# Turning x before the weights in the norm blocks of a twelve-stage decoder

## The reference

```python
def _layernorm(x, axis=-1, eps=1e-05):
    m = jnp.mean(x, axis=axis, keepdims=True)
    v = jnp.var(x, axis=axis, keepdims=True)
    return (x - m) / jnp.sqrt(v + eps)
```

## Time and profile before

| what | value |
|---|---|
| median of 3 runs | 2674.46 us (2674.36 to 2676.65) |
| time of the profiled execution | 2665.88 us |
| its span, first to last instruction | 2664.1 us |
| mean granted clock of PE over the span | 0.897 |
| PE busy | 2126.5 us, 80% |
| DVE busy | 1709.5 us, 64% |
| ACT busy | 1191.6 us, 45% |
| POOL busy | 588.5 us, 22% |

### The profile page before, as it was taken

How to read it: one execution, slowest core, us unless ns; L and a number is a source line. 1 busy time by engine, 2 the same in 40 slices (tenths; PEclk the granted TensorE clock), 3 DMA queues, 4 the chain that set the end, 5 groups by cost and what they waited for, 6 DMA issues and landing times. The chain is left out here.

```text
span 2664.1 us, 28164 instructions
## 1 busy us (share of the span) xinstructions
PE 2126.5 (80%) x10151; PEld 1326.3 (50%) x10181; DVE 1709.5 (64%) x2541; ACT 1191.6 (45%) x1889; POOL 588.5 (22%) x344
## 2 busy tenths in 40 slices
PE   5789889694699979979694888888778989272895
PEld 3456556584323325767541444444555654251574
DVE  5555455324677745632287999999845767857765
ACT  2334322100266653411065999999822236312330
POOL 3331112120242103012101756564101200000100
PEclk8889999697799998969897999999879989696996
DMA  6553120343554400034400000000111000000001
GB/s 125 86 88 41 61 95 0 107 158 126 101 79 64 48 20 2 1 108 161 131 32 32 1 1 1 0 1 1 65 59 36 1 1 0 0 8 21 0 1 38
DMA packets 107525, 126.69 MB, mean 48 GB/s; under 512 B 14823, under 2 KB 98676, under 8 KB 106357
## 3 DMA queue, kind: packets, MB, share of 16 engines
q1 hardware_dynamic: 96790, 110.17, 17.9%
q10 hardware_dynamic: 7712, 7.17, 0.9%
q0 software_dynamic: 2880, 7.48, 0.8%
HBM read 91.11 MB, written 33.29 MB: 47 GB/s over the span
## 5 line engine op out<-in xcount | busy, mean ns | idle before, releaser
L3274 DVE TENSOR_TENSOR_SCAN l2s_h<-l2w_aw 128x2048 f32<-128x2048 f32 x64 | 290.0, 4531 | 5.4 <-ACT l2s_rs L3394 5.4
L3202 PE MATMUL l2s_big<-g_xn,g_ident 128*128 128x512 f32 x512 | 258.4, 607 | 11.6 <-ACT g_xn L3387 6.4
L3358 POOL TENSOR_SCALAR l2w_aw<-l2w_aw 128x2048 f32<-128x2048 f32 x64 | 212.1, 3314 | 141.4 <-DVE l2w_aw L3266 136.2
L591 DVE TENSOR_REDUCE l1at_nm<-l1at_s 128x1 f32<-128x512 f32 x256 | 161.8, 683 | 65.3 <-PE l1at_s L441 64.4
L3194 PE MATMUL l2s_c_ps<-g_ident,l2s_h 128*128 128x128 f32 x1024 | 148.9, 279 | 55.7 <-ACT g_xn L3387 36.4
L3194 PEld LDWEIGHTS l2s_c_ps<-g_ident,l2s_h 128*128 128x128 f32 x1024 | 117.1, 141 | 146.8 <-issue 87.8
L691 ACT ACTIVATE g_xn<-l1at_s 128x512 f32<-128x512 f32 x256 | 143.5, 598 | 82.1 <-PE l1at_s L465 81.3
L3387 ACT ACTIVATE g_xn<-l2s_c_ps,l2s_ct 128x512 f32<-128x512 f32 x256 | 163.1, 690 | 15.9 <-PE l2s_c_ps L3194 15.7
L3380 ACT ACTIVATE l2w_aw<-l2s_dt,l2w_A 128x2048 f32<-128x2048 f32 x64 | 128.3, 2006 | 0.0
L591 DVE TENSOR_REDUCE l0at_nm<-l0at_s 128x2 f32<-128x384 f32 x128 | 69.7, 556 | 91.3 <-PE l0at_s L441 90.2
L3202 PEld LDWEIGHTS l2s_big<-g_xn,g_ident 128*128 128x128 f32 x512 | 82.0, 190 | 81.9 <-ACT g_xn L3387 59.2
(11 more groups left out here) (868 smaller groups left out, 4872.2 us busy)
## 6 DMA issues: line engine op xcount, KB each, us to landing
l1f_w<-in_L_ffn_w_dram SPq DMA_DIRECT2D x16, 1024.0 KB
l0f_w<-L_ffn_experts_inter_dram SPq DMA_DIRECT2D x7, 1024.0 KB
l0f_w<-n_L_ffn_experts_out_dram SPq DMA_DIRECT2D x7, 1024.0 KB
l0at_qs<-l0at_parts SPq DMA_DIRECT2D x18, 256.0 KB, 9.2
l0at_ks<-l0at_parts SPq DMA_DIRECT2D x18, 256.0 KB, 18.2
l1at_qs<-l1at_parts SPq DMA_DIRECT2D x18, 256.0 KB, 8.9
l1at_ks<-l1at_parts SPq DMA_DIRECT2D x18, 256.0 KB, 20.2
expert_rows<-g_zeros SPq DMA_DIRECT2D x1, 4096.0 KB, 12.8
```

The costliest lines, as they stand in the source:

```text
L591: V.tensor_reduce(nm[:, s % 2, qts[0]:qts[-1] + 1, r], s1[:, u % 3, 0:len(qts) * KEYS].rearrange("p (q k) -> p q k", k=KEYS), AX, ALU.max, ...
L3202: nc.tensor.matmul(acc[:, tb, :], ident[:], hCT[:, tb, :], start=n == 0, stop=n == NST - 1).then_inc(acc_done, 1)
L3274: V.tensor_tensor_scan(out=h_all[:, i % 2].rearrange("p c t -> p (c t)"), data0=dA[:, i % 2].rearrange("p c t -> p (c t)"), data1=wd[:, i ...
L3358: nc.gpsimd.tensor_scalar(wd[:, i % 3], wd[:, i % 3], 10.0, -10.0, ALU.min, ALU.max).then_inc(clipped, 1)
```

## The change

PE's list now has the pairs of x first and the groups of weights after them; ACT's list has, after the square root, its copies of the turned x first and those of the weights after them. Nothing is added or removed, and DVE, SP and the DMAs issued stay as they are. In l1a and l3c, without groups, the instruction lists are the same as before.

```diff
--- before.py
+++ after.py
@@ -274,15 +274,13 @@
                 for r in range(rounds):
                     act.wait_ge(var_ready, r + 1)
                     nc.scalar.activation(tmp[:], tmp[:], ACT.Sqrt).then_inc(std_ready, 1)
+                copy_turned(act, nc.scalar.copy, 0)
                 copy_blocks(act, nc.scalar.copy, groups, wt, wt_ready, wt_copied, 0, 1)
-                copy_turned(act, nc.scalar.copy, 0)
                 if loads[1::2]:
                     act.wait_ge(loaded[1], 16 * len(loads[1::2]))
 
             @block.tensor
             def _(pe):
-                turn_blocks(nc, pe, groups, wt, ident, loads, loaded, wt_ready, [wt_copied])
-
                 for g in range(TILES // 2):
                     pe.wait_ge(xn_ready, 2 * g + 2)
                     if g >= 4:
@@ -291,6 +289,7 @@
                         for v in range(2):
                             ins = nc.tensor.transpose(pt[:, g % 4, 2 * kc + v, :], xn[:, 2 * g + v, kc * P:(kc + 1) * P], ident[:])
                     ins.then_inc(tr_ready, 1)
+                turn_blocks(nc, pe, groups, wt, ident, loads, loaded, wt_ready, [wt_copied])
```

## The result

The changed kernel takes 2677.44 us (median of 22 runs, 2672.59 to 2686.59). The kernel before, run beside it, takes 2672.30 (22 runs, 2666.12 to 2677.30), which is 2.16 less than the 2674.46 of its first three runs. The ratio is 1.0020, with a 95% interval from 1.0014 to 1.0027: +5.1 us, between +3.7 and +7.2. It is slower, as forecast, but by half of the +10.6.

A forecast was written before the change was run, and what follows sets the result against it. DVE was taken to set the end of most norm blocks, hiding the weights' work. Upper-clock block terms of +6.57 us plus +4.0 for the clock gave +10.6 on 2674.46, so 2685.0 us, range 2678.0 to 2692.5.

The forecast's parts named there:

- Who ends a block, and that its end is paid: Norm blocks: DVE's last copy ends them, +8.36 after its first tensor_scalar; lengthening a block's last instruction is paid in full.
- The terms at the upper clock: Block-end changes with fast PE: l0a +2.48, l2a +4.21, l3a +0.99, l3b +0.50, l1b -1.61; sum +6.57 us.
- The 0.166: Spacing in us between starts of ACT's weight copies, read from l0a's 16 copies and used for l0a, l3a, l3b, l1b.
- I take two of five, +4.0: PE's clock in the five changed blocks: two run their last pairs at the lower clock, adding 4.0 us.
- The price: Cost of PE's lower clock in and behind one changed block, taken as 2.0 us.
- caught: State of a block whose last pairs PE turns at the lower clock; one to three such blocks forecast, chance 0.50.
- an even coin: Of l1a and l3c, blocks with the same lists, one had the lower clock; used as odds for the five changed blocks.
- the 2610.2 of the prediction: Time in l3c when PE's granted clock rose, about 2610.2 us, at the end of the first 20 transpositions.
- The base: Whole kernel: the blocks' terms were added to the median of runs before the change, 2674.46 us.
- The case of all five at the upper clock: Rival for the five changed blocks: none at the lower clock, +6.6 us, 2681.0 us; chance 0.20.
- Loads that land later in l1b: Rival: later landings in timed runs slow only the old order, up to 3.57 us in l1b; chance 0.10.
- The clock under transpositions: Norm blocks: a skill rule says transposing never raises the clock, so all five lag; l2a's trace disagreed, no share given.

The follow-up runs named there:

- ACT's list alone: Kernel before with ACT copying x ahead of the weights in l0a, l3a and l3b, PE's list unchanged; run twice, ratios 0.9997 and 1.0011.
- the filler: Kernel before with twenty transpositions of the identity put ahead of the pairs in l1a; ratio 1.0007.
- l1b alone: Kernel before with x ahead of the weights only in block l1b, on PE and ACT; ratio 0.9999.
- the caught one: Second run of the kernel before with x first only in l1b and the weights' copies there shared by ACT and DVE; ratio 0.9989.
- The second look at the changed kernel: The changed kernel run and profiled once more, unchanged, timed against the kernel before; ratio 1.0022.
- l2a alone: Kernel before with x ahead of the weights only in block l2a, on PE and ACT; run twice, ratios 1.0031 and 1.0021.
- l2a copied twice: Kernel before with x first only in l2a, and ACT copying each of its 28 weight blocks twice, first into a spare tile; ratio 1.0037.

## Why the prediction was wrong, point by point

**Who ends a block, and that its end is paid.** Right for the end of the block. In all thirteen profiles every block in the old order, l1b and l1a apart, ends at +8.36 to +8.38; ACT's copies behind it move the end one for one, and the next block's first instruction with it. "Paid in full" is not shown for the whole program: with ACT's list alone, both profiles had 1.6 of the 2.7 us back by the end.

**The terms at the upper clock.** Right, within 0.3 in each block and 0.4 in the sum (6.57 forecast, 6.16 read). l3a is the largest miss: four of its seven copies are of 128x64 and start 0.11 apart. The 0.166 itself has a wait in it: between the twelfth and the thirteenth copy of l0a before the change (15.36 to 15.65) ACT had nothing to copy yet. In the changed l0a the 16 copies start 0.157 apart (22.11 to 24.46). That the forecast for l0a is exact is therefore part luck, as its last copy lasted 0.46 and not 0.30.

**"I take two of five, +4.0."** This is the step that failed. The price was near (1.72 in the block against 2.0 taken; the 0.3 for what comes behind is not shown), how often it happens was not: in both profiles of the changed kernel the term is 0. In all profiles together, 16 blocks with weights ran with x first (five each in two profiles of the changed kernel, one each in six others), and one was caught. It is one of five in l1b and none of eleven in the other four. l3c, of the same shape, was at the upper clock for its last pairs in all thirteen. l1a is the odd one: its last pairs ran at the lower clock throughout in ten of thirteen, at the upper one in two, and fell between with the filler. I took one block of each kind for an even coin and spread it over five others; four of them behave like l3c, and l1b nearly does. With 1 in 16 the term is 5 x 0.06 x 2.0, some 0.6, and the forecast would have been +7.2 us, at the upper end of the interval.

The rows also show how near l1b is to being caught. Its last pairs start at +6.07. PE's stretch in the changed kernel's first profile, and in the profile with l1b alone:

```profile
1004.00:1005.00 1.00, 0.33 (x2) 0.65 0.00 0
...
```

```profile
1002.00:1003.00 1.00, 0.33 (x3) 0.78 0.00 0
...
```

A granted clock of 0.65 over a microsecond that begins at 0.50 means a rise at 1004.7, or +5.7; the other is +5.8. In the five profiles with x first in l1b the rise comes at +4.8, +5.5, +5.7, +5.8 and, in the caught one, +9.6; in the other four blocks at +4.1 to +5.1. So l1b escaped by 0.4 and 0.5 us in the changed kernel's two profiles, and that it escaped in both is partly luck. The same working puts l3c's rise at 2610.36, +5.4, while PE waited for DVE, and not at the 2610.2 of the prediction.

The second look at the changed kernel, in which l1a itself was at the upper clock (its last 12 took 1.51), shows that nothing in the block's list decides it. Why l1a differs stays open. It is alone in having its loads at full rate as PE starts (381 GB/s in 662.5 to 663.0), but that doesn't hold the clock down by itself: in the two profiles in which l1a was at the upper clock the loads ran at 385 and 389 GB/s as PE started, and with the filler the clock rose under 383. No run varied the stages ahead of l1a.

**The base.** Adding to the median of three runs put the forecast 2.16 too high; with the base of 22 runs it would have been 2682.9. Both errors have the same sign, and so the time fell just under the range's lower end of 2678.0. The case of all five at the upper clock (2681.0, +6.6) is the one that both profiles of the changed kernel show; it had been given 0.20. How many blocks were caught in the 22 timed runs isn't known, as only one of them has a profile.

**The rivals.** Loads that land later in l1b: in the eight profiles that had the old order there, PE started on the weights at +3.75 to +3.96, so landing scatters by 0.2 us, not by the microseconds that the rival needed. The block's end scatters more, +12.85 to +13.50, but that is the clock: it rose at +8.65 in the profile whose block ended first and at +9.85 in the one whose block ended last, while PE was turning weights and x. The clock under transpositions: in 15 of the 16 blocks with x first PE did nothing but transpositions and its last 12 took 1.50 to 1.51, at the upper level. In the changed l0a PE had run nothing at all before them. The Trainium skill's rule ("TensorE: Matmul & The Clock Gate", "Part 4: PE-mode transpose"), by which the clock would stay down, disagrees with that, and the measurement decides.

**What stays open.** The timed +5.1 is 1.1 under the blocks' sum, within its interval, and l2a alone timed above its block in both runs. Whether a shifted start moves the clock's falls in later stages with some system, or they just scatter, can't be told from the intervals. The profiles speak for some of both. The last stage is 59.2 us in eleven and 57.6 in the two with ACT's list alone. From l3b's `tensor_scalar` to l3c's it is 146.2 to 146.4 us in seven of the nine profiles with l3b's block as before, and 142.9 and 143.1 in the other two, one of them the first profile of the kernel before; less the block's own 0.44, the changed kernel took 145.7 both times. The 2.8 us that it seemed to lose there is thus a short stretch in the profile it was held against.

## What to carry to other kernels

Before moving work out of the head of a list, ask what it is hidden behind: if another engine (here DVE, in five blocks of six with the same +8.36) sets the end anyway, the head is free and the tail is not. An order that pays where a load is late (l1b) costs where it isn't, so choose it by block. When a term hangs on a state that two blocks show differently, count it over several executions before giving it a weight.

## What the runs showed of the hardware that was not expected

A granted clock that falls at another moment can cost more than the change under study: in the last part of a cross-attention one execution lost 5.9 us to another with the same instructions. A clock that is up can also fall while PE is at work: in l1a with the filler it fell at 665.2, half a microsecond after PE had come back from an idle time of 2.04 us (0.62 in 665 to 666 above). That idle time alone does not bring it down, as in l0a, in the second profile of the kernel before and four others, PE idled the same 2.04 us and the clock stayed up. The rise can come while PE waits, as it did in l1b and l3c. And ACT's copies of 128x128 from PSUM start 0.157 us apart, and those of 128x64 0.11, where PE is ahead of them, even where the shown duration of one grows from 0.27 to 0.99 us (l2a copied twice): read the distance of starts, not the duration.
